# Two-layer conditioned attention block on one core: columns on ScalarE's queue, the first weight by halves, and the last turned probabilities ahead of the values' projection

## The reference

```python
xn = layer_norm(x, norm_w, norm_b)
q, k, v = xn @ q_w + q_b, xn @ k_w + k_b, (xn @ v_w + v_b) * mask
# layer 0: 16 heads, softmax(q k^T + mask_bias) @ v
# layer 1: 8 heads, q softmax over features, k softmax over tokens, q @ (k^T v)
scale, shift = split(silu(cond) @ emb_w + emb_b)
h = layer_norm(y, sb_norm_w, sb_norm_b) * (1 + scale) + shift
x = x + silu(h) @ out_w + out_b
```

## Time and profile before

| | |
|---|---|
| time, median of 3 runs | 1098.57 us (1097.37 to 1098.67) |
| profiled execution | 1097.78 us, span 1096.0 us |
| PE busy | 1054.8 us (96% of the span) |
| DVE busy | 759.8 us (69%) |
| ACT busy | 591.6 us (54%) |
| POOL busy | 448.6 us (41%) |
| granted TensorE clock, mean | 0.993 |
| DMA | 71.65 MB, mean 65 GB/s |

### The profile page before, as it was taken

How to read it: one execution, slowest core, us unless ns; L and a number is a source line. 1 busy time by engine, 2 the same in 40 slices (tenths; PEclk the granted TensorE clock), 3 DMA queues, 4 the chain that set the end, 5 groups by cost and what they waited for, 6 DMA issues and landing times. The chain is left out here.

```text
span 1096.0 us, 25953 instructions
## 1 busy us (share of the span) xinstructions
PE 1054.8 (96%) x8696; PEld 909.8 (83%) x8696; DVE 759.8 (69%) x1326; ACT 591.6 (54%) x1960; POOL 448.6 (41%) x783
## 2 busy tenths in 40 slices
PE   6999999999999999999999999999999999999995
PEld 4878888888888888888887778888888888888884
DVE  4656766676666766667678787777777777777764
ACT  5366667776677766776588443433343443434431
POOL 3242434334343343433343344444444444444432
PEclk9999999999999999999999999999999999999997
DMA  8824110111101111011102211111111111111011
GB/s 275 256 84 141 42 61 24 62 62 41 60 24 62 62 41 59 25 62 63 43 23 98 95 50 33 40 55 57 57 57 57 57 57 57 52 52 39 31 38 58
DMA packets 46017, 71.65 MB, mean 65 GB/s; under 512 B 10256, under 2 KB 14448, under 8 KB 45968
## 3 DMA queue, kind: packets, MB, share of 16 engines
q1 hardware_dynamic: 45968, 71.02, 20.3%
HBM read 54.19 MB, written 16.79 MB: 65 GB/s over the span
## 5 line engine op out<-in xcount | busy, mean ns | idle before, releaser
L1276 PE MATMUL bank<-xt_hi,w_hi 128*128 128x256 f32 x768 | 228.4, 297 | 3.1 <-DVE xt_lo L893 3.1
L1277 PE MATMUL bank<-xt_lo,w_hi 128*128 128x256 f32 x768 | 218.5, 284 | 0.0
L1278 PE MATMUL bank<-xt_hi,w_lo 128*128 128x256 f32 x768 | 218.3, 284 | 0.0
L454 POOL TENSOR_SCALAR stat<-stat 128x1 f32<-128x1 f32 x128 | 34.5, 270 | 441.8 <-DVE stat L884 417.7
L613 ACT ACTIVATE prob<-prob,neg_max 128x128 f32<-128x128 f32 x512 | 198.7, 396 | 6.7 <-DVE neg_max L907 6.6
L632 ACT ACTIVATE th<-z_s 128x512 f32<-128x512 f32 x64 | 40.5, 633 | 249.9 <-POOL z_s L488 249.8
L1276 PE MATMUL bank<-w_hi,xt_hi 128*128 128x512 f32 x384 | 158.3, 412 | 1.0 <-DVE w_lo L835 1.0
L1276 PEld LDWEIGHTS bank<-xt_hi,w_hi 128*128 128x128 f32 x768 | 148.9, 194 | 9.1 <-DVE w_lo L835 4.8
L1278 PE MATMUL bank<-w_hi,xt_lo 128*128 128x512 f32 x384 | 150.5, 392 | 0.0
L1277 PE MATMUL bank<-w_lo,xt_hi 128*128 128x512 f32 x384 | 149.8, 390 | 0.0
L1277 PEld LDWEIGHTS bank<-xt_lo,w_hi 128*128 128x128 f32 x768 | 148.6, 193 | 0.0
(11 more groups left out here) (130 smaller groups left out, 2203.3 us busy)
## 6 DMA issues: line engine op xcount, KB each, us to landing
x_in<-in_x_dram SPq DMA_DIRECT2D x32, 256.0 KB, 2.8
x_res<-in_x_dram SPq DMA_DIRECT2D x32, 256.0 KB, 2.9
between_layers<-x_res SPq DMA_DIRECT2D x32, 256.0 KB, 2.0
x_in<-between_layers SPq DMA_DIRECT2D x32, 256.0 KB, 2.8
x_res<-between_layers SPq DMA_DIRECT2D x32, 256.0 KB, 2.8
out_dram<-x_res SPq DMA_DIRECT2D x32, 256.0 KB, 2.6
room<-in_L_cond_W_emb_dram SPq DMA_DIRECT2D x8, 512.0 KB, 7.3
prob<-in_L_cond_emb_w_dram SPq DMA_DIRECT2D x4, 512.0 KB, 7.5
```

Source lines behind the costliest of these rows:

```text
L454: pool.tensor_scalar(v[:, 8:9], v[:, 7:8], EPS, None, ALU.add).then_inc(s[a_in].sem, 1)
L1276: pe.matmul(o, a_hi, b_hi, start=start, stop=False)
L1277: pe.matmul(o, a_hi, b_lo, start=False, stop=False)
L1278: return pe.matmul(o, a_lo, b_hi, start=False, stop=stop)
```

## The change

Four edits:

- **Columns.** The six columns of layer 0 (normalisation weight and bias, the query and key biases, the second norm's weight and bias) are issued by ScalarE on its own queue, as the first things in its list, and no longer by SP.
- **First weight.** Its two halves signal two semaphores. ScalarE and TensorE's bias part wait for each half where they need it. High parts 0 to 3 now all stand ahead of `xt_high(0)`, on VectorE the low parts likewise.
- **A guard.** VectorE's waits for `mask_saved` and `film_dve` ahead of `film_scale(0, k, 0)` stand in step 0 and no longer in step 13.
- **Order on TensorE.** In `step0` and `step_mixed`, `turn_probs(k, 1, (2, 3))` goes ahead of the values' projection, and `weigh(k, 1)` ahead of `turn_yn(k, 0)`.

```diff
+        def weight_in(l, j, i):
+            if (l, j) == (0, WQ):
+                return (w_first, w_in[0][WQ])[i], 16
+            return w_in[l][j], 32
...
             def start():
                 load_front(0, pair(0))
-                load_norm(0)
                 load_weight(0, WQ)
                 load_weight(0, WK)
                 load_wide(0, WV, VALUE_BIAS[0])
-                load_col(0, QB, WQ, par_in[0])
...
-                load_col(0, KB, WK, par_in[0])
...
-                for i, name in ((W2, "w2"), (B2, "b2")):
-                    load_col(0, i, name, par_in[0])
...
         @block.scalar
         def _(act):
-            act.wait_ge(consts, 1)
+            def load_columns():
+                for i, name, signal in ((NW, "nw", norm_in[0]), (NBI, "nb", norm_in[0]), (QB, WQ, par_in[0]),
+                                        (KB, WK, par_in[0]), (W2, "w2", par_in[0]), (B2, "b2", par_in[0])):
+                    act.dma_start(col[:, 0, i, :], columns(0, name), allow_slow_non_contiguous=True).then_inc(signal, 16)
...
             def high_part(l, j, some=range(C)):
-                act.wait_ge(w_in[l][j], 32)
                 act.wait_ge(norm_in[l], 16 * 2)
...
                 for c in some:
+                    if c % 2 == 0:
+                        act.wait_ge(*weight_in(l, j, c // 2))
...
-                high_part(0, WQ, (0, 1))
+                high_part(0, WQ)
                 xt_high(f, 0, 0)
-                high_part(0, WQ, (2, 3))
                 xt_high(f, 0, 1)
...
+            load_columns()
+            act.wait_ge(consts, 1)
             start()
...
                 if i == G - 3:
                     bias_col(1, WK, KB, 6)
+                if i == 0:
                     dve.wait_ge(mask_saved, 16)
                     dve.wait_ge(film_dve, 3)
                 film_scale(0, k, 0)
...
                 keys(0, f, slot, 1)
+                turn_probs(k, 1, (2, 3))
                 values(0, FIRST, f, slot, 0)
...
-                turn_probs(k, 1, (2, 3))
+                weigh(k, 1 - slot, 1)
                 turn_yn(0, k, 0)
-                weigh(k, 1 - slot, 1)
...
                 y_rows(k, 0)
+                turn_probs(k, 1, (2, 3))
                 values(1, MIXED, f, slot, 1)
-                turn_probs(k, 1, (2, 3))
+                weigh(k, 1 - slot, 1)
                 turn_yn(0, k, 0)
-                weigh(k, 1 - slot, 1)
```

More of the change, by code:

```diff
@@ L210, in build @@
         w_in = [[sem(f"w_in{l}{j}") for j in range(4)] for l in range(2)]
+        w_first = sem("w_first")
         w_high = [[sem(f"w_high{l}{j}") for j in range(4)] for l in range(2)]
@@ L260, in build, with columns @@
         LAST0 = At(None, B - 1)
+        def weight_in(l, j, i):
+            if (l, j) == (0, WQ):
+                return (w_first, w_in[0][WQ])[i], 16
+            return w_in[l][j], 32
+        def columns(l, name):
+            v = layers[l]["b"][name] if isinstance(name, int) else layers[l][name]
+            return v.rearrange("(c p) -> p c", p=P)
         def sequence(dram, at):
@@ L280, in load_col @@
             def load_col(l, i, name, signal):
-                v = layers[l]["b"][name] if isinstance(name, int) else layers[l][name]
-                sp.dma_start(col[:, l, i, :], v.rearrange("(c p) -> p c", p=P),
-                             allow_slow_non_contiguous=True).then_inc(signal, 16)
+                sp.dma_start(col[:, l, i, :], columns(l, name), allow_slow_non_contiguous=True).then_inc(signal, 16)
             def load_norm(l):
@@ L295, in load_weight @@
                 for i in range(2):
-                    sp.dma_start(raw[l][j][i], rows[i]).then_inc(w_in[l][j], 16)
+                    sp.dma_start(raw[l][j][i], rows[i]).then_inc(weight_in(l, j, i)[0], 16)
             def load_emb(l, some):
@@ L1016, in start @@
                 spread_norm_b(0)
-                low_part(0, WQ, (0, 1))
+                low_part(0, WQ)
                 xt_low(f, 0, 0)
-                low_part(0, WQ, (2, 3))
                 xt_low(f, 0, 1)
@@ L1228, in bias_part @@
                 pe.wait_ge(spread, l + 1)
-                pe.wait_ge(w_in[l][j], 32)
                 for c in range(C):
+                    if c % 2 == 0:
+                        pe.wait_ge(*weight_in(l, j, c // 2))
                     last = pe.matmul(bank[b][32 * c:32 * (c + 1), :], norm_b_32[:, c, :], raw[l][j][c // 2][:, c % 2],
```

## The result

The changed kernel takes 1129.11 us (median of 6 runs, 1128.15 to 1132.02) against 1098.62 us for the kernel before (6 runs, 1096.48 to 1099.16). The ratio is 1.0285, with a 95% interval from 1.0271 to 1.0299: it is 2.9% slower. The forecast was 1131, with a range of 1117 to 1147.

The account below looks back on a forecast made before the run. TensorE, busy 33.88 of a step's 34.43 us, was taken as the bound: 1097.8 + 30.0 (steps 0 to 14) + 3.6 (step 15) - 1.3 (start) = 1130.1, or 1131 us as the median, range 1117 to 1147.

Parts of the forecast that it names:

- The bound: Layer 0: TensorE sets the step's time; the 6.46 us chain from `turn_yn(k, 0)` to `output(k, 0)` has no slack.
- The wait at group 3: Steps 0 to 14: early `turn_probs` of group 3 would wait 0.88 us for ScalarE's last exponentials.
- A step: Steps 0 to 14: `turn_yn(k, 0)` and everything behind it come 2.00 us later, +30.0 us over 15 steps.
- The wait at `output`: Steps 0 to 14: TensorE would stand 1.88 us ahead of `output(k, 0)` for VectorE's `s_lo`.
- The copies' wait at `weigh`: Steps 0 to 14: the 0.45 us wait for ScalarE's copies of the turned probabilities, 6.8 us in all, would vanish.
- Step 15: Last step of layer 0: group 3 still waits until 598.82, values and `weigh` follow, `turn_yn` comes 3.6 us later.
- The start: Before step 0: the first projection, at 15.02, would come 1.3 us earlier, the middle of 0.4 and 2.2.
- The halves: Start: ScalarE's 1.28 us table load comes behind the weight's first half only, so some 1.2 us is covered.
- The columns: Start: SP issues the first weight 1.03 us sooner, against four more columns beside x and weight costing 1.8 us uncovered.
- Earlier if the columns hide: Start: first projection 2.2 us earlier if the columns' traffic fits the idle share of the DMA stretch.
- The clock rival: Layer 0: longer waits also lower TensorE's clock, 1.7 us a fall; 1144 us if half of 16 steps fall; chance 0.27.
- The faster rival: Steps 0 to 14: chain shrinks to 4.6 us or less and group 3's wait vanishes, giving 1084 us; chance 0.05.

Follow-up runs that it names:

- turns_early: Changed kernel with `turn_yn(k, 0)` ahead of `weigh(k, 1)` again, only `turn_probs(k, 1, (2, 3))` staying early; 1113.03 us, ratio 1.0151 to the kernel before.
- weigh_first: Changed kernel with `turn_probs(k, 1, (2, 3))` behind the values again, only `weigh(k, 1)` moved ahead of `turn_yn(k, 0)`; 1134.39 us, ratio 1.0339 to the kernel before.
- s_low_first: Changed kernel with VectorE's `s_low_part(k, 0)` ahead of `y_norm(k, 1)` and its moments; 1136.22 us, ratio 1.0356 to the kernel before.
- order_only: Kernel before with only TensorE's new order, the start and guard as before; 1130.18 us, ratio 1.0303.
- split_norm: halves_only with the moments of sequence 1 moved behind `s_low_part(k, 0)` on VectorE; 1092.89 us, ratio 0.9953 to the kernel before.
- split_norm_turn: split_norm with `turn(n, 0)` ahead of `weigh(k, 1)` on TensorE in steps 0 to 14; 1092.56 us, ratio 0.9957 to the kernel before.
- halves_only: start_only with all six columns back at their old places on SP's queue, the weight's halves kept; 1096.33 us, ratio 0.9994 to the kernel before.
- norm_columns: TensorE's old order, the weight's halves, and only the two norm columns on ScalarE's queue; 1094.82 us, ratio 0.9977 to the kernel before.
- columns_only: start_only with the old waits and order for the first weight, the six columns staying on ScalarE's queue; 1096.42 us, ratio 0.9994 to the kernel before.
- start_only: Changed kernel with TensorE's old order in all steps; columns, halves and guard stay; 1096.13 us, ratio 0.9989 to the kernel before.

## Why the prediction was right, point by point

- **The bound** (all of the step's time is TensorE's work or its waits; `output(k, 0)` already starts on `s_lo`): right. turns_early and weigh_first each delay `turn_yn` by one cause, 0.95 and 2.07 us, and each step follows by 1.03 and 2.12. s_low_first, which brings `s_lo` 0.76 earlier, takes 0.76 from `output`'s wait.
- **The wait at group 3**: predicted to start 0.06 behind the end of the exponentials, measured 0.05; the profile shows 0.71 of it as idle, where I counted 0.88 from start to start.
- **A step**: predicted +2.00, measured +2.09 in steps 2 to 12. Of this `turn_yn` has 2.05. What `turn_yn` has beyond 2.00 is a slightly longer lead of values into `weigh` (369.17 - 366.23 = 2.94, where I took 2.85). The wait at `output` was to be 1.88; the profile shows 1.78 of idle time.
- **Steps 0 and 1**: I took 2.0 for each. Step 0 lost 1.34 (0.63 in order_only), though it has both waits; why it lost less I leave open. Step 1 lost 3.49, 1.4 of it clock.
- **The copies' wait at `weigh`**: gone, as predicted.
- **Steps 13 and 14**: I took 2.0 for each. Step 13 lost 1.82. Step 14 lost 1.36: `bias_part` of 1 us stands ahead of `keys` there, so the exponentials are done and group 3 does not wait. This makes the sum 0.6 smaller.
- **Step 15**: `turn_yn` +3.6 as predicted, the step itself +3.1.
- **The start**: predicted -1.3 at the first projection, measured -1.33, and -1.15 to -1.47 in the other six profiles with this start. The halves: 1.2 foreseen, 1.37 and 1.39 measured in split_norm and split_norm_turn (2.07 in the lucky profile of halves_only). The columns: I took the middle between 1.03 won and 0.8 lost, 0.1 won; measured is 0.1 lost (13.72 against 13.64), with halves_only as the measure 0.8. The forecast is right here, but two steps behind it are not borne out. "Earlier if the columns hide" was no real bound: no kernel with the columns moved came near 2.2, and of the 1.03 us that SP issues earlier at most 0.4 arrived at the landing of the first half. And the price of 0.46 for each of four extra columns is not seen: norm_columns does without them and is no earlier. That DMAs issued by different engines interleave, as the Trainium skill says (DMA: Bandwidth & Descriptors, "Issuing engines are not separate DMA queues"), agrees with x at 3.93 in columns_only against 3.42. The gain of only 0.4 that I drew from it did not come about.
- **The guard**: no part of the difference is seen at it (step 13 takes 36.09 us in the kernel before and 36.11 in start_only, which has the guard moved); it was not tried alone.
- **The clock rival** (0.27): not in steps 2 to 15 of the changed kernel's profile, whose clock there was 1.00, but real. Step 1 lost 1.4 us to it (mean clock 0.92 against 0.95 before; 0.92 in order_only and weigh_first too), and one of the six runs of the changed kernel, 1132.02 us, has a mean clock of 0.989 where the others have 0.991 or 0.992. weigh_first, with waits of 0.89 and 1.79 a step, had a fall in the middle of layer 0, and its runs spread by 8.8 us with their mean clock.
- **The faster rival** needed a chain of 4.6 us or less: it stayed at 6.51.
- **The sum**: for the profiled execution 1130.1 predicted, 1128.15 measured. That it is so near is in part luck: the chance of the clock at the start took off about 2.2, steps 0, 13, 14 and 15 another 1.9 together, while step 1 and steps 2 to 12 put back 2.4.

## What to carry to other kernels

A wait of 0.45 us that stands out in the list of waits can be the cheap end of something longer: before moving work ahead of an instruction, follow what its result sets off on the other engines and compare that chain with the work left in front of the place where it comes back. Here 6.46 us of chain stood against 6.21 us of list (`weigh`, its wait and 4.58 of work), and one microsecond of `weigh` put in front cost one microsecond a step. When two arms of a chain meet at the same moment, the part to shorten is the one behind their meeting; moving the moments from behind the silu to behind `s_lo` took 0.76 us from `output`'s wait in the changed kernel. Of that only 0.2 a step was left, because the moments that were pushed back made the next operand, `yn` of sequence 1, come just too late, and the return of the loop came to light: behind one end of a chain the next stands close by.

## What the runs showed of the hardware

- The same start code ran its first projection at the pace of TensorE's upper clock in one execution (matmuls of 256 columns 0.12 us apart from 13.69) and not in another (0.21 apart from 13.80, until 18.4), while the profile's clock column read 1.00 in both. For small gains at a start, one profile says little: here such chance was worth more than the edit.
- Waits of 0.89 and 1.79 us in each step, with dense work between, were followed by a fall of the clock to 1.2 GHz in one of steps 2 to 12 in weigh_first's profile and in none of them in the changed kernel's, with 0.71 and 1.78. With one profile of each, this tells of chance as much as of the waits.
- Loads from one queue landed up to 0.7 us apart in profiles with the same order of issues (the first half of the weight 4.1 us behind its issue in halves_only, 4.8 and 4.7 in split_norm and split_norm_turn).
- Two column loads of 2 KB on a second queue, beside 512 KB of x on the first, with the first weight issued 1.03 us sooner behind it, went with x at 4.26 and not at 3.29 to 3.49. The second of six such columns landed 6.0 us after its issue in the changed kernel.
- At the return of TensorE's hardware loop 0.30 to 0.46 us of idle time show up in the kernels whose last operand of a step comes 0.14 to 0.23 us ahead of its use, and none where it comes 1.05 us or more ahead.
